# Experts' bias: from a product on TensorE per tile to an addition on VectorE, and later weights' low parts spread over six tiles

## The reference

```python
    gate_logits = xf @ gate_w.T + gate_b
    gates = jax.nn.softmax(gate_logits, axis=-1)
    selected = jnp.argmax(gates, axis=-1)
    out = jnp.zeros((xf.shape[0], expert_w.shape[1]), dtype=xf.dtype)
    for j in range(expert_w.shape[0]):
        yj = xf @ expert_w[j].T + expert_b[j]
        out = out + jnp.where((selected == j)[:, None], yj, 0.0)
...
x = x + jnp.tanh(g_ffn[1]) * _L1_ffn_ref(_layernorm(x, axis=-1), ...)
```

## Time and profile before

| what | value |
|---|---|
| median of 3 runs | 793.2 us (792.78 to 797.03) |
| the profiled execution's own time | 797.66 us |
| its span, first to last instruction | 795.9 us |
| PE busy | 755.1 us (95% of the span) |
| DVE busy | 459.6 us (58%) |
| ACT busy | 430.5 us (54%) |
| POOL busy | 274.5 us (34%) |
| mean granted clock of TensorE | 0.982 of full speed |

### The profile page before, as it was taken

One profiled execution on the slowest core, in us unless ns is written; L12 is line 12 of the kernel. 1 busy time (PEld: TensorE's weight loads), 2 busy tenths in 40 slices (PEclk: granted clock), 3 DMA queues, 4 the chain that ended last, 5 costly groups with the idle time before them and its releaser, 6 DMA issues.

```text
span 795.9 us, 12734 instructions
## 1 busy us (share of the span) xinstructions
PE 755.1 (95%) x3975; PEld 592.2 (74%) x3975; DVE 459.6 (58%) x1038; ACT 430.5 (54%) x1274; POOL 274.5 (34%) x431
## 2 busy tenths in 40 slices
PE   5999989899999999999999999999999987987997
PEld 3888877788888888888888888888887743555775
DVE  4786411556465656564655565656558764787652
ACT  4543315556556556555655655655555466557831
POOL 0331005234334233424423523433322438624242
PEclk9999999999999999999999999999999999797999
DMA  8545461132041140140131203203142135664232
GB/s 303 180 133 172 133 189 46 49 150 76 15 173 37 57 173 28 54 183 15 66 119 80 66 30 158 80 15 120 34 131 85 54 109 184 240 261 158 73 109 76
DMA packets 42126, 87.82 MB, mean 110 GB/s; under 512 B 5561, under 2 KB 26041, under 8 KB 38226
## 3 DMA queue, kind: packets, MB, share of 16 engines
q1 hardware_dynamic: 38884, 78.71, 28.7%
q0 software_dynamic: 3184, 8.41, 3.1%
HBM read 70.28 MB, written 35.57 MB: 133 GB/s over the span
## 4 chain that ended last, share of the span: by engine, by line
PE 71%; DVE 6%; ACT 3%; POOL 2%; DMA 2%; issue 1%; POOLq 0%; DVEq 0%; SPq 0%
PE banks L882 8%; PE banks L916 7%; PE banks L884 7%; PE banks L883 7%; PE banks L918 7%; PE banks L917 7%; PE banks L868 6%; PE banks L903 3%; PE banks L895 2%; PE banks L1831 2%; PE banks L1830 2%; PE banks L1832 2%; PE banks L927 2%; PE banks L929 2%; PE banks L928 2%
## 5 line engine op out<-in xcount | busy, mean ns | idle before, releaser
L592 ACT ACTIVATE p_sb<-p_sb,nmax 128x128 f32<-128x128 f32 x256 | 99.7, 391 | 62.7 <-DVE nmax L784 62.5
L587 ACT ACTIVATE oT_hi<-banks 128x512 fp32r<-128x512 f32 x64 | 38.2, 597 | 140.1 <-PE banks L929 140.1
L822 DVE SCALAR_TENSOR_TENSOR x_sb<-banks,tgates,x_sb 128x512 f32<-128x512 f32 x64 | 48.0, 749 | 70.8 <-PE banks L918 70.8
L690 POOL TENSOR_TENSOR v_lo<-v_raw,v_hi 128x128 fp32r<-128x128 f32 x64 | 29.5, 461 | 133.6 <-ACT v_hi L635 133.6
L779 DVE SCALAR_TENSOR_TENSOR p_sb<-banks,q_rstd,mask 128x128 f32<-128x128 f32 x256 | 71.5, 342 | 4.5 <-POOL q_rstd L83 4.0
L868 PEld LDWEIGHTS banks<-kT,qT_sb 128*128 128x128 f32 x512 | 67.7, 193 | 5.9 <-issue 0.5
L695 POOL TENSOR_TENSOR p_sb<-p_sb,rsum 128x512 f32<-128x512 f32 x64 | 66.5, 1040 | 15.2 <-DVE rsum L812 15.2
L868 PE MATMUL banks<-kT,qT_sb 128*128 128x128 f32 x512 | 68.2, 277 | 0.1
L768 DVE TENSOR_TENSOR oT_lo<-banks,oT_hi 128x512 fp32r<-128x512 f32 x64 | 44.1, 689 | 33.0 <-ACT oT_hi L587 33.0
L400 PE MATMUL banks<-w_hi,ctx_hi 128*128 128x512 f32 x128 | 54.1, 422 | 9.0 <-DVE ctx_lo L331 9.0
L816 DVE TENSOR_TENSOR pT_lo<-banks,pT_hi 128x512 fp32r<-128x512 f32 x64 | 44.2, 690 | 24.9 <-ACT pT_hi L610 24.9
(11 more groups left out here) (276 smaller groups left out, 1901.9 us busy)
## 6 DMA issues: line engine op xcount, KB each, us to landing
sorted_x<-in_empty SPq DMA_DIRECT2D x8, 2064.0 KB, 9.7
w_raw<-in_wq_l SPq DMA_DIRECT2D x8, 1024.0 KB, 5.1
w_raw<-in_wo_l SPq DMA_DIRECT2D x8, 1024.0 KB, 4.8
exp_w<-in_exp_w_l SPq DMA_DIRECT2D x8, 1024.0 KB, 9.3
kT_scr<-kT_st SPq DMA_DIRECT2D x16, 256.0 KB, 2.3
v_scr<-v_st SPq DMA_DIRECT2D x16, 256.0 KB, 2.3
xs<-sorted_x SPq DMA_DIRECT2D x15, 258.0 KB, 2.8
v_raw<-v_scr SPq DMA_DIRECT2D x14, 256.0 KB, 2.6
```

The source lines that it names most:

```text
L592: last = act.activation(p_sb[:, b % 2, h * P:(h + 1) * P], p_sb[:, b % 2, h * P:(h + 1) * P], ACT.Exp, bias=nmax[:, b % 2, h:h + 1], accum ...
```

## The change

The bias product on PE, its high and low parts, their zeroed table and all the transfers and waits for them go. SP loads in their place the biases of all experts on all partitions, `s.bias`, 128 x 4096 values (2 MB), as soon as the last row has been updated. DVE gets a new stage `add_bias(t)`, which adds gate times bias to `xs` in place, between `split_x` and `add_y`; `add_y` comes after it and is unchanged. For tiles 8 to 14, `add_bias` reads the expert's number into a register of DVE's queue. The 16 later pieces of the weights, up to now four per turn in four turns, are now three per turn in five turns and one in a sixth (`later_chunks`), starting two turns earlier on each of ACT and DVE.

```diff
@@ block.sync of experts
             sp.wait_ge(s.recycled, 1)
-            sp.wait_ge(bias_zeroed, 1)
-            sp.dma_start(s.exp_b2[0:2, :, :].bitcast(F32), d.exp_b2).then_inc(exp_b_ld, 16)
+            sp.wait_ge(x3_done, B)
+            sp.dma_start(s.bias[:, :, :], d.exp_b).then_inc(bias_ld, 16)
             sp.wait_ge(scattered, 16 * B)
+        def later_chunks(t):
+            return [divmod(c, KT) for c in range(READY * KT + 3 * t, min(READY * KT + 3 * t + 3, E * KT))]
@@ block.scalar
-            act.wait_ge(gateT_done, 2)
-            act.activation(s.exp_b2[:, :, :], s.zero[:, 0:1].unsqueeze(2).to_broadcast([P, E, D]), ACT.Copy)\
-                .then_inc(bias_zeroed, 1)
...
             def split_next_w(t):
-                if READY <= t < E:
-                    split_w(t)
-
-            run([(normalise, 2), (split_x, 1), (split_next_w, 3)])
+                for n, kt in later_chunks(t):
+                    e = ORDER[n]
+                    act.activation(s.ew_hi[:, e, kt, :], s.exp_w[:, e, kt, :], ACT.Copy).then_inc(w_hi_done, 1)
+
+            for e in range(HB):
+                act.wait_ge(s.exp_ld[e // 2], 32)
+            run([(normalise, 2), (split_x, 1), (split_next_w, 1)])
@@ block.vector
+            def add_bias(t):
+                slot = t % SLOTS
+                dve.wait_ge(xn_done, t + 1)
+                if t == 0:
+                    dve.wait_ge(bias_ld, 16)
+                if t < E:
+                    e = ORDER[t]
+                else:
+                    if t == E:
+                        dve.wait_ge(tile_done, 1)
+                    e = dve.value_load(tile_i[0:1, t - E:t - E + 1], min_val=0, max_val=E - 1)
+                dve.scalar_tensor_tensor(out=xs[:, slot, 0:D], in0=s.bias[:, e, :], scalar=s.tgates[:, 3:4],
+                                         in1=xs[:, slot, 0:D], op0=ALU.mult, op1=ALU.add).then_inc(bias_added, 1)
+
             def add_y(t):
                 slot = t % SLOTS
                 dve.wait_ge(y_done, t + 1)
+                dve.wait_ge(bias_added, t + 1)
...
             def split_next_w(t):
-                if READY <= t < E:
-                    split_w(t)
-
-            run([(split_x, 1), (add_y, -1), (split_next_w, 2)])
+                for n, kt in later_chunks(t):
+                    e = ORDER[n]
+                    dve.wait_ge(w_hi_done, KT * n + kt + 1)
+                    dve.tensor_tensor(s.ew_lo[:, e, kt, :], s.exp_w[:, e, kt, :], s.ew_hi[:, e, kt, :].bitcast(F32),
+                                      ALU.subtract).then_inc(w_lo_done, 1)
+
+            run([(split_x, 1), (add_bias, 1), (add_y, -1), (split_next_w, 0)])
@@ block.tensor, multiply
-                if t == 0:
-                    pe.wait_ge(exp_b_ld, 16)
-                pe.matmul(out, s.ones_r[:, :], s.exp_b2[:, e, :], start=True, stop=False)
...
-                    pe.matmul(out, xsT_hi[:, t % 2, cols], s.ew_hi[:, e, kt, :], start=False, stop=False)
+                    pe.matmul(out, xsT_hi[:, t % 2, cols], s.ew_hi[:, e, kt, :], start=(kt == 0), stop=False)
@@ kernel inputs
-    d.exp_b, d.exp_w = a["exp_b"], a["exp_w_l"]
+    d.exp_b, d.exp_w = a["exp_b"].to_broadcast([P, E, D]), a["exp_w_l"]
```

More of the change, by code:

```diff
@@ L543, in loads @@
                 sp.dma_start(wo_raw[:, :, :], d.wo[g, :, :, :]).then_inc(wo_ld, 16)
-                if isinstance(g, int) and g == 1:
-                    sp.dma_start(s.exp_b[:, :], d.exp_b).then_inc(s.exp_b_ld, 16)
                 v_half(0)
@@ L572, in _ @@
             fill(0)
-            sp.wait_ge(s.exp_b_split, 2)
-            sp.dma_start(d.exp_b2[0], s.exp_b_hi[:, :].bitcast(F32)).then_inc(s.exp_b_stored, 16)
-            sp.dma_start(d.exp_b2[1], s.exp_b_lo[:, :].bitcast(F32)).then_inc(s.exp_b_stored, 16)
             sp.wait_ge(q_done, 8 * G - 8)
@@ L645, in q_seed @@
                 act.activation(seed[:, c, :], lnss[:, c, :], ACT.Exp, scale=-0.5).then_inc(seed_done, 1)
[L647 to L650, removed]
             def seed_ln2(u, b, g, odd):
@@ L660, in copy_xT @@
                 if after(u, b, g, HB - 1):
-                    act.wait_ge(s.exp_b_stored, 32)
                     for n in (0, 1, 2):
@@ L681, in _ @@
             run(act, [(oT_split, -2), (qT_copy, 5), (square, 5)] + weights
-                + [(exps, 0), (q_seed, 4), (pT_split, -1), (v_split, 2), (split_bias, 0)],
+                + [(exps, 0), (q_seed, 4), (pT_split, -1), (v_split, 2)],
                 [(oT_split, -2), (qT_copy, 5), (square, 5), (pT_split, -1), (v_split, 2), (exps, 0), (q_seed, 4), (copy_z01, 0),
@@ L754, in _ @@
             dve.memset(s.gate_c[:, :, :], 0.0).then_inc(s.ones_set, 1)
-            dve.memset(s.zero[:, :], 0.0).then_inc(s.ones_set, 1)
-            dve.wait_ge(s.ones_set, 3)
-            dve.tensor_copy(s.ones_r[:, :], s.ones[:, :]).then_inc(s.ones_set, 1)
             for k in range(EXTRA):
@@ L830, in x_stats @@
                         layernorm_var(dve, s, x_step, 2 * (b + 1), slice(b + 1 - HB, b + 1)).then_inc(xval_done, 1)
[L832 to L836, removed]
             def copy_xT(u, b, g, odd):
                 if after(u, b, g, HB - 1):
-                    dve.wait_ge(s.exp_b_stored, 32)
                     for n in (3,):
@@ L854, in _ @@
             run(dve, [(oT_split, -2), (mask_max, 0), (pick_sums, 4), (q_half, 4), (p_recip, 0), (pT_split, -1),
-                      (accumulate, -2), (x_stats, -2), (split_bias, 0)],
+                      (accumulate, -2), (x_stats, -2)],
                 [(oT_split, -2), (mask_max, 0), (normalise_ln2, -4), (pT_split, -1), (pick_sums, 4), (q_half, 4),
@@ L1267, in _ @@
             dve.wait_ge(s.gate_ld, 16 * GATE_LOADS)
-            dve.wait_ge(s.ones_set, 4 + EXTRA)
+            dve.wait_ge(s.ones_set, 2 + EXTRA)
             dve.scalar_tensor_tensor(out=s.gate_c[:, :, 0:E], in0=sm_ps[:, 320:320 + E].unsqueeze(1).to_broadcast([P, KT, E]),
@@ L1384, in _ @@
             pe.wait_ge(s.gate_ld, 16 * GATE_LOADS)
-            pe.wait_ge(s.ones_set, 4)
+            pe.wait_ge(s.ones_set, 2)
             for kt in range(KT):
@@ L1443, in experts @@
         w_hi_done, w_lo_done = m.sem("ew_hi_done"), m.sem("ew_lo_done")
-        exp_b_ld, bias_zeroed = m.sem("exp_b2_ld"), m.sem("bias_zeroed")
+        bias_ld, bias_added = m.sem("bias_ld"), m.sem("bias_added")
         y_done, res_done = m.sem("ey_done"), m.sem("eres_done")
@@ L1858, in flamingo @@
     d.fold, d.empty = a["fold"], a["empty"].rearrange("(p k) n -> p (k n)", p=P)
-    d.exp_b2 = nc.dram_tensor("exp_b2", (2, E, D), F32, kind="Internal").ap()
     d.eid, d.base = a["iota"].to_broadcast([P, E]), a["base"].to_broadcast([P, E])
@@ L1938, in flamingo @@
             s.ctx_res, s.xln3, s.prod = beside("ctx_res", [P, B, D], 0), beside("xln3", [P, HB, D], 16), beside("prod", [P, 2, D], 24)
-            s.exp_b2, s.xn = beside("exp_b2", [P, E, D], 0, F32R), beside("xn", [P, 2, D], 24)
+            s.bias, s.xn = beside("exp_bias", [P, E, D], 0), beside("xn", [P, 2, D], 24)
             s.x3T = [s.at(f"x3T{c}", [P, KT, HALF], 8 * c) for c in range(2)]
@@ L1980 @@
         "exp_w_l": i["L1_ffn_expert_w"].reshape(E, D, KT, P).transpose(0, 3, 2, 1),
-        "exp_b": i["L1_ffn_expert_b"],
+        "exp_b": i["L1_ffn_expert_b"].reshape(1, E, D),
         "ident": np.eye(P, dtype=np.float32),
```

7 lines of the change are left out of this document (1 added, 6 removed).

## The result

The changed kernel took 796.49 us (median of 20 runs), the kernel before 793.65 (20 runs). The ratio is 1.0034, with a 95% interval of 1.0018 to 1.0051: slower by 2.7 us (1.4 to 4.0). The forecast was +0.4 within a range of 789.6 to 797.2, and no change beyond 0.5%; the ratio keeps within both, at 0.34%. The loss is small, but the measurement tells it from none.

The account below looks back on a forecast made before the run. PE bounds the kernel, with DVE's turn and the reload loop close behind. These eat PE's 3.5 us gain; the last `add_y` comes 0.4 us later, so 793.2 + 0.4 = 793.6 us, range 789.6 to 797.2.

Parts of the forecast that it names:

- DVE's turns: On DVE, turns 1 to 4 take 3.73 us against PE's new 3.23, so DVE sets the pace in turns 1 to 5.
- The addition: `add_bias` on DVE, between `split_x` and `add_y`: 0.66 us from start to start, bounds 0.60 and 0.75.
- The gain of 3.5 us on PE: Fifteen bias products leave PE at 0.233 us each; the whole gain if PE stays the bound.
- the reload loop: Tile t+6's load waits for tile t's store; each round passes three tiles and grows by 0.66 us, from tile 8 by 0.96.
- the rival of slow stores: On POOL, the addition makes every store slow: 795.7 us, or 796.9 with prices at upper bounds; chance 0.12.
- the read on DVE: Loading the expert's number into DVE's register in tiles 8 to 14: 0.3 us taken, bounds 0 and 0.66.
- The end of the sum: From tile 14's transposes to the last `add_y`, PE leads again: 6.67 us before, 6.21 less two bias products.
- The store of tile 4: On POOL, 2.46 us before against 0.98 for tile 5; its slow round of 11.62 us was carried over, plus 0.96.
- The quick rounds: Reload rounds from `add_y(t)` to `add_y(t+3)` grow from 9.54 to 10.5 us, 3.50 a tile, over PE's 3.23.
- PE staying the bound: Rival: PE runs on as the bound in the loop over tiles, giving 789.7 us; chance 0.15.
- the rule of the Trainium skill: DVE and GpSimd share a port pair, locked for a whole instruction, so the addition can hold up a store.
- The late table: Rival: the 2 MB bias table lands late, counting from 25 us after issue; at 30 us, 798.6 us; chance 0.03.

Follow-up runs that it names:

- the thirteenth product: Changed kernel with one more product per tile put back on PE, output unchanged: ratio 1.0031 with six slots of `xs`, 0.9992 with seven.
- the slot: Changed kernel with seven slots of `xs` in place of six, nothing else changed: ratio 0.9957, loop 51.31 us.
- the order of two lines on DVE: Changed kernel with `add_bias` moved behind `add_y` on DVE, same instructions: ratio to the kernel before 0.9986, loop 54.11 us.
- the register read first: Changed kernel with PE reading the expert's number of tiles 8 to 14 ahead of its wait for the rows' low part: ratio 1.0022, loop 55.45 us.
- all three repairs: Changed kernel with seven slots, `add_bias` behind `add_y`, and PE's read of the expert's number ahead of the wait: ratio 0.9968, loop 51.27 us.
- POOL's addition: Changed kernel with seven slots, POOL adding the bias in place of DVE, ACT scaling the table by the gate once: ratio 0.9973, loop 52.10 us.

## Why the prediction was right, and where its sum was off

*The place and the kind of the loss* were as forecast. DVE's turns: 3.73 us forecast, 3.73 measured. The addition: 0.66 and 0.66. `add_y(4)`: 1.83 us late forecast, 1.53 measured, or 1.79 when the earlier start of the loop by 0.26 is taken off. The table of biases: DMA moved 168 GB/s in 712 to 716 us and 358 in 716 to 720, where it moved 0 and 6 before, together about the 2 MB of the table, and nearly the same as before in 720 to 724 (202 against 198); so it was there some 18 us ahead of its first reader at 738.01. The gain of 3.5 us on PE was eaten: shown by the thirteenth product. That the reload loop ate it, and not DVE's work as such: shown by the slot, and by the order of two lines on DVE. PE waited for the rows' low part in tiles 4 to 7 and in 8 and 11 to 13 (there with the register's read behind it), much as stated.

*The range held partly by luck.* The forecast's own steps had a range of 792.0 to 794.8 us, and 796.49 lies above it. It lies below 797.2 because that end was set by the rival of slow stores with all prices at their upper bounds, and that rival did not happen. Only 0.45 of the 2.9 us over the forecast come from the kernel before, whose median is now 793.65 and not 793.2.

*The size* was off: +0.4 in the sum, +2.4 in the loop. Four terms:

- **The register on PE**, which the step on the reload loop left out. I priced the read on DVE (0.3 forecast; 0.54 in tile 8 by the starts of `split_x` and `add_bias`, then 0.14 to 0.29) and forgot that PE reads the same number behind the same wait, though the earlier trace rows show it. I had PE start tile 12 0.05 us after its low part; it took 1.35, while the low part itself was done 0.72 earlier than forecast. Reading first gave back 1.06 us.
- **The end of the sum**, where I let PE lead from the transposes of tile 14 on, 6.21 us to the last `add_y`. It took 7.23, and 7.20 with the register read first. I had followed one round, through tiles 7 and 10, to the end, and left out the one beside it, from `add_y(8)` to the load of tile 14. ACT's list has the high part of tile 13 behind `xn` of tile 14, so tile 13 hangs on that round as well.
- **The store of tile 4** was quick (0.98 us). In that turn DVE had only one low part left to make, and it was over before the store began; the round from `add_y(4)` to `add_y(7)` took 11.01 us and not 12.58, a miss in the other direction of 1.57.
- **The quick rounds** were not 10.5 us but 11.50 from `add_y(7)` and 12.41 from `add_y(8)`. The stores of tiles 7 and 8 landed 3.2 and 3.8 us after their issue. The median of the stores after 760 us was 2.7 before, 3.2 in the changed kernel and 2.6 to 2.9 in the variants. It isn't this execution alone: the round from `add_y(8)` took 11.60 with the register read first and 12.03 with six slots and 13 products, against 10.82 before. Why was not tested, and stays open.

The loop took 2.0 us more than forecast, and the kernel with the register read first tells how they divide. Up to the transposes of tile 14 the forecast had 48.34 us from the loop's start; the changed kernel took 49.28, and with the register read first 48.25. So the sum up to there is right but for PE's read, with the quick store and the slower rounds cancelling each other, which is luck. Behind them the other 1.0 is lost in both kernels. With the register read first its cause is seen: PE waits 0.64 us for the low part of tile 13, and `xn` of tile 14 came 8.87 us after `add_y(8)`, where the forecast reckoned 7.60 for such a stretch. This rests on one execution of each.

*The rivals.* PE staying the bound (0.15) did not happen with six slots, and did with seven, from tile 7 on. The slow stores (795.7 us, so near the measured time) did not come: most stores took 0.98 us, not about 2, and those beside low parts took 1.86 instead of 2.46. What the runs show of the rule of the Trainium skill named there ("SBUF — State Buffer", on the two separate sides) is told in the last section. The late table did not occur.

A version that beats both kernels is the changed one with seven slots: 792.37 us, ratio 0.9957 (0.9933 to 0.9981); the one with all three repairs can't be told from it. The seven slots fit, since seven slots of 2064 bytes end below the 16 KB at which `ew_hi` begins.

## What to carry to other kernels

Before work is taken off the fullest engine, look how far the next bound is: here a loop of store, reload and normalise ran at 3.18 us a tile against PE's 3.47. Taking 0.23 off PE left 0.06 us between the two, and the addition put 0.22 a tile into the loop, so the product removed from PE counted for next to nothing. In a kernel with rotating buffers, write down one round of a buffer with every instruction that stands ahead of its members on each engine, and put new work behind the member that frees the buffer; or give the ring one buffer more. Put a read into a register ahead of the wait for data, not behind it: behind it, it costs nothing while the data are early, and its full time (about 1 us here) once they are late. And follow every one of the interleaved rounds to the end, not only one.

## What the runs showed of the hardware

Some stores on POOL wait for DVE's operations with two inputs in SBUF. In the changed kernel the store of tile 0 starts at 746.04, DVE's three low parts end with the start of `split_x` at 746.95, and the store ends at 747.90, 0.95 later, which is a whole undisturbed store: as if it had begun its work only when DVE's run was over. The three after it do the same, and so does the first store with the addition behind `add_y`: DVE's low parts end at 743.93, the store (742.37, 2.52 us) at 744.89. Five stores, in four kernels, began during an `add_bias` and took 1.3 us.

Yet the first four stores of the kernel without addition took 1.25 us beside such a run, and ten more in six other kernels 1.25 to 1.28. Low parts start 0.60 us apart and the run began 0.90 before the store, so the third one starts 0.30 after it, and 0.30 + 0.95 is 1.25: as if these stores had waited for one low part and not for the run. The rule named above, a lock for one whole instruction, fits this group and the 1.3 us; in the first group the wait lasted for the whole run. The scatter in the earlier trace rows took 0.97 beside low parts and did not wait at all. Which of the three a store falls into no run here tells.

The other way round, POOL's addition, with two inputs in SBUF, doubled the time of DVE's low parts: two runs of three took 3.79 and 3.75 us, against 1.89 and 1.88 beside a store alone. The additions overlapped these two runs by 1.78 and 1.71 us, about what the runs grew by, so DVE stood still for the most of them, and the additions were not themselves stretched (1.3 us). This too looks like a lock for one whole instruction.
